# A four-layer graph network on one core: the same operations in new orders on all engines, with new PSUM banks

## The reference

```python
x = _layernorm(x + L0(x, nodemask, adj, adj, W_qkv, W_out, b_out))   # attention
x = _layernorm(x + L1(x, adj, W1, b1, gamma, beta, W2, b2))          # hypergraph convolution, twice
x = _layernorm(x + L2(x, adj, Wv, bv, aw, ab, Wk, bk))               # gated transition, applied K-1 times
x = _layernorm(x + L3(x, adj, W))                                    # mean over neighbours, then a linear map

# L0, 8 heads of 64
attn = softmax(where(m2, q @ k.T * scale, -big)) * 0.33
attn = attn + 0.33 * where(m2, adj, 0) + 0.33 * exp(-where(m2, adj, big))
out  = (attn @ v) @ W_out + b_out
# L1: conv(z, W, b) = Dn * (H @ (Be * (H.T @ (z @ W.T)))) + b, H = (adj != 0)
h = layer_norm(relu(conv(x, W1, b1)), gamma, beta); out = conv(h, W2, b2) + x
# L2
e = leaky_relu(sj + si + ab); T = adj * exp(e) / rowsum
out = relu(x @ Wk[0] + (T @ x) @ Wk[1] + (T @ T @ x) @ Wk[2] + sum(bk))
# L3
out = relu(concat(x, (adj @ x) / deg) @ W.T)
```

## Time and profile before

| | us |
|---|---|
| median of 3 runs | 1377.84 |
| lowest and highest run | 1376.25, 1380.79 |
| profiled execution, device time | 1377.72 |
| its span, first to last instruction | 1375.8 |
| PE busy | 1290.7 (94%) |
| DVE busy | 1075.6 (78%) |
| ACT busy | 956.0 (69%) |
| POOL busy | 550.1 (40%) |

### The profile page before, as it was taken

One profiled execution on the slowest core, in us unless ns is written; L12 is line 12 of the kernel. 1 busy time (PEld: TensorE's weight loads), 2 busy tenths in 40 slices (PEclk: granted clock), 3 DMA queues, 4 the chain that ended last, 5 costly groups with the idle time before them and its releaser, 6 DMA issues.

```text
span 1375.8 us, 32640 instructions
## 1 busy us (share of the span) xinstructions
PE 1290.7 (94%) x9577; PEld 1111.6 (81%) x9577; DVE 1075.6 (78%) x3291; ACT 956.0 (69%) x2806; POOL 550.1 (40%) x1221
## 2 busy tenths in 40 slices
PE   4799999999999999999999999999999999999985
PEld 3678888888888888888888888888888888888863
DVE  2568878888887887887888878888888778888873
ACT  3467767777777777777777777677777777777753
POOL 3034434344443444443334444344444434444432
PEclk8899999999999999999999999999999999999997
DMA  6000000000000000000000010000001000000000
GB/s 192 11 16 25 24 16 16 23 17 24 24 15 24 16 21 19 24 24 15 24 16 16 24 24 20 19 16 23 17 24 24 15 24 16 19 21 24 16 8 8
DMA packets 44292, 32.51 MB, mean 24 GB/s; under 512 B 8176, under 2 KB 43120, under 8 KB 44272
## 3 DMA queue, kind: packets, MB, share of 16 engines
q1 hardware_dynamic: 42688, 31.47, 8.1%
q0 software_dynamic: 176, 0.52, 0.2%
q10 hardware_dynamic: 1408, 0.27, 0.1%
HBM read 23.87 MB, written 8.39 MB: 23 GB/s over the span
## 4 chain that ended last, share of the span: by engine, by line
PE 29%; POOL 22%; issue 19%; DVE 16%; ACT 9%; POOLq 1%; ACTq 1%; DVEq 0%; DMA 0%; SPq 0%
POOL rs L1520 9%; PE PS L400 4%; PE PS L522 4%; PE PS L401 4%; PE PS L404 4%; POOL rs L1526 3%; POOL rs L1516 3%; DVE ysb L1287 3%; PE PS L532 3%; POOL ys L1533 3%; ACT qk L817 2%; DVE ysb L1279 2%; DVE st L1291 2%; DVE ys L1169 2%; POOL gate L1541 2%
## 5 line engine op out<-in xcount | busy, mean ns | idle before, releaser
L1520 POOL TENSOR_TENSOR rs<-rs,mhalf 128x1 f32<-128x1 f32 x320 | 180.0, 562 | 25.4
L834 ACT ACTIVATE prob<-PS,neg_max 128x128 f32<-128x128 f32 x512 | 179.5, 413 | 1.8 <-DVE neg_max L1145 1.8
L1158 DVE SCALAR_TENSOR_TENSOR prob<-prob,rl,gate 128x128 f32<-128x128 f32 x512 | 160.1, 372 | 0.2
L852 ACT ACTIVATE x<-ysb,rs 128x256 f32<-128x256 f32 x128 | 78.3, 612 | 104.3 <-POOL rs L1526 104.3
L478 PE MATMUL PS<-xT_hi,wqk_hi 128*128 128x256 f32 x512 | 139.5, 294 | 9.0 <-DVE wk_lo L1071 4.8
L1574 POOL TENSOR_TENSOR z<-z,bk_bc 128x256 f32<-128x256 f32 x64 | 48.1, 751 | 236.7 <-ACT z L902 236.7
L479 PE MATMUL PS<-xT_hi,wqk_lo 128*128 128x256 f32 x512 | 136.4, 287 | 0.0
L834 ACT ACTIVATION_READ_ACCUMULATOR prob<-PS,neg_max 128x1 f32 x512 | 129.8, 253 | 0.0
L1516 POOL TENSOR_TENSOR rs<-mv,eps_c 128x1 f32<-128x1 f32 x256 | 54.2, 212 | 186.3 <-DVE mv L1081 186.3
L1192 DVE SCALAR_TENSOR_TENSOR hid<-PS,Dn,b_bc 128x512 f32<-128x512 f32 x64 | 48.1, 751 | 82.8 <-PE PS L404 82.8
L478 PEld LDWEIGHTS PS<-xT_hi,wqk_hi 128*128 128x128 f32 x512 | 99.9, 195 | 11.3 <-issue 5.0
(11 more groups left out here) (213 smaller groups left out, 4280.8 us busy)
## 6 DMA issues: line engine op xcount, KB each, us to landing
xin<-in_x_dram SPq DMA_DIRECT2D x32, 256.0 KB, 2.8
out_dram<-xout SPq DMA_DIRECT2D x32, 256.0 KB, 2.2
adj_in<-in_adj_dram SPq DMA_DIRECT2D x32, 128.0 KB, 2.1
wrow<-in_adj_dram SPq DMA_DIRECT2D x32, 128.0 KB, 4.6
wqkv_raw<-in_L_gnn_W_qkv_dram SPq DMA_DIRECT2D x1, 1536.0 KB, 7.7
w_raw<-in_L_gnn_W_dram SPq DMA_DIRECT2D x3, 512.0 KB, 11.9
mask_bc<-in_nodemask_dram SPq DMA_DIRECT2D x32, 32.0 KB, 2.9
wk_raw<-in_L_gnn_Wk_dram SPq DMA_DIRECT2D x3, 256.0 KB, 8.7
```

What stands on the lines that cost most here:

```text
L834: last = act.activation(prob[:, t, h, :], PS[:, bank, k * P:(k + 1) * P], ACT.Exp, bias=neg_max[:, t, h:h + 1], accum_out=row_sum[:, t, h: ...
L852: act.activation(dst, src, ACT.Identity, scale=rs[:, n, g, 1:2], bias=rs[:, n, g, 0:1]).then_inc(done, 1)
L1158: last = dve.scalar_tensor_tensor(prob[:, t, h, :], prob[:, t, h, :], rl[:, t, h:h + 1], gate[:, t], ALU.mult, ALU.add)
L1520: return pool.tensor_tensor(rs[:, n, g, 1:2], rs[:, n, g, 0:1], mhalf[:], ALU.pow)
```

## The change

All 23 settings of PSUM banks are new. The order of items changes in group on PE, ACT, DVE and POOL; SP's is as it was. No item is added or dropped, and no item's own code changes. Waits of the form after(...) are dropped where they were for the old banks and others are put in for the new ones. The diff, cut to its core:

```diff
-        bank_adjT = 7
-        bank_xT0 = 7
-        bank_qk = (0, 3, 1, 7)
-        bank_v = (3, 0)
-        bank_S = (1, 5)
+        bank_adjT = 4
+        bank_xT0 = 1
+        bank_qk = (3, 0, 0, 2)
+        bank_v = (4, 5)
+        bank_S = (6, 2)
...
-        bank_h = (6, 4)
-        bank_hT = (0, 4)
-        bank_y1 = (4, 0)
+        bank_h = (2, 5)
+        bank_hT = (1, 1)
+        bank_y1 = (0, 6)
...
 # PE
                 if B:
-                    after(pe, dve_o3, 2, s - 2, 2)
                     h_(j, 0)
-                if F:
+                    h_(j, 1)
+                if F:
+                    after(pe, dve_hb, 2, s - 1, 1)
                     qk_(i, 3)
                 if B:
-                    h_(j, 1)
-                if F:
-                    after(pe, act_qk, 4, s, 3)
+                    hT_(j, 0)
+                if F:
                     S_(i, 0)
-                if B:
-                    hT_(j, 0)
-                if F:
                     S_(i, 1)
                 if B:
+                    after(pe, dve_hT, 2, s - 1, 1)
                     hT_(j, 1)
                     hw_(j, 0)
                     hw_(j, 1)
                     y1_(j, 0)
+                    after(pe, act_exp, 4, s, 2)
                     y1_(j, 1)
-                if F:
-                    v_(i, 0)
-                    after(pe, dve_y1, 2, s - 1, 2)
-                    v_(i, 1)
                 if L:
                     xT0_(n)
+                if F:
+                    v_(i, 0)
+                    v_(i, 1)
                 if B:
                     xT2_(j)
...
                 if F:
                     PV_(i, 0)
                 if B:
+                    after(pe, act_E, 4, s - 1, 4)
                     T1_(j, 0)
+                if F:
+                    after(pe, dve_xT0, 1, s + 1, 1)
+                    PT_(i, 1)
+                if B:
+                    T1_(j, 1)
                 if L:
-                    after(pe, act_E, 4, s - 1, 4)
-                    after(pe, act_v, 2, s, 2)
                     qk_(n, 0)
                 if B:
-                    T1_(j, 1)
-                if F:
-                    PT_(i, 1)
-                if B:
-                    after(pe, act_qk, 4, s + 1, 1)
                     T2_(j, 0)
+                if F:
+                    PV_(i, 1)
+                if B:
+                    T2_(j, 1)
                 if L:
                     qk_(n, 1)
-                if B:
-                    T2_(j, 1)
-                if F:
-                    after(pe, dve_o2, 2, s - 1, 1)
-                    PV_(i, 1)
+                if F:
+                    after(pe, dve_OT, 2, s, 1)
                     W_(i, 0)
...
 # DVE, after the first hb_
                     hb_(0)
-                    hb_(1)
                     bnh_(0)
                     mvh_(0)
+                    hb_(1)
+                    hT_(0)
+                    degb0_()
+                    bnh_(1)
                 if F:
                     max_(0)
...
 # POOL
                 if B:
                     resid_(0)
                     resid_(1)
+                    rsh_(0)
+                    aT_()
+                if F:
+                    fresid_()
+                if B:
+                    rsh_(1)
                 if F:
                     gate_()
-                if B:
-                    rsh_(0)
-                    rsh_(1)
-                    aT_()
-                if F:
-                    fresid_()
```

More of the change, by code:

```diff
@@ L684, in group @@
                 if F:
-                    after(pe, act_exp, 4, s, 2)
+                    after(pe, act_exp, 4, s, 4)
                     PT_(i, 0)
@@ L938, in group @@
                 if B:
-                    relu_(j, 0)
-                    aT_(j)
+                    hT_(j, 0)
                 if F:
@@ L973, in group @@
                 if B:
-                    al_(j, 1)
+                    Z01_(j, 1)
                     Y_(j, 0)
-                if L:
-                    qk_(n, 0)
-                if B:
-                    Y_(j, 1)
                 if F:
@@ L982, in group @@
                 if B:
-                    x3_(j, 0)
+                    Y_(j, 1)
+                if L:
+                    qk_(n, 0)
                 if F:
                     OT_(i, 1)
+                    carry(i)
+                if B:
+                    x3_(j, 0)
                 if L:
@@ L1348, in group @@
                 if B:
-                    hT_(0)
-                    bnh_(1)
                     mvh_(1)
                     hT_(1)
+                    degb_()
                     hw_(0)
@@ L1376, in group @@
                 if F:
-                    Dsum_(0)
+                    norm_(1, 0)
                 if B:
                     Z_(0)
-                if L:
-                    front(n)[1]()
                 if F:
+                    rl_(1, 1)
                     norm_(1, 1)
@@ L1385, in group @@
                     gmax_(0)
+                    al_(0)
                     Z_(1)
[L1387 removed]
+                if L:
+                    after(dve, pe_v, 2, s, 2)
+                    front(n)[1]()
+                if B:
+                    all_(0)
                     z2_(0)
[L1389 to L1390 removed]
                     gmax_(1)
                     al_(1)
+                    z2_(1)
                     den_(0)
                     rden_(0)
+                    all_(1)
                     Y_(0)
[L1396 removed]
+                    den_(1)
+                    rden_(1)
+                    Y_(1)
+                    Yl_()
                 if F:
@@ L1441, in group @@
                     y3_(0)
-                    o3_(1)
-                    bn3_(0)
-                    mv3_(0)
-                    y3_(1)
                 if F:
@@ L1448, in group @@
                 if B:
+                    bn3_(0)
+                    o3_(1)
+                    mv3_(0)
+                    y3_(1)
                     bn3_(1)
```

109 lines of the change are left out of this document (49 added, 60 removed).

## The result

The changed kernel takes 1362.93 us (median of 4 runs, 1359.42 to 1364.37), the kernel before 1379.05 us beside it (4 runs, 1376.25 to 1380.79): a ratio of 0.9881 with a 95% interval of 0.9855 to 0.9908. A second measurement gave 0.9889 (0.9868 to 0.9910). So it is 16 us faster where 9 were forecast; 1363 lies in the range of 1350 to 1391. The profiled execution took 1362.91 with a span of 1361.1; that of before had 1375.8, so 14.7 us are to be found.

What follows compares the result with a forecast made beforehand. It took a latency cycle through all engines, meeting an almost full PE, as the bound. The last gain to bind, 0.28 us a pass over 31 passes, made 8.7 us: 1377.8 - 8.7 = 1369, range 1350 to 1391.

Steps and rivals of the forecast that it cites:

- Step 1: End of the pass on DVE: bn3_(0) ahead of o3_(1) brings mv3_(0) about 0.3 us earlier, out_(j, 1) near 3.2.
- Step 7: Middle and end of the pass: new waits end 0.1 to 0.5 us before PE comes; T3_, ax_ keep their distance.
- Steps 2 and 3: Heads of ACT and PE: relu_(j, 0) directly behind mask_, hT_(j, 0) before S_; hT_(j, 1) at 8.97, gain 0.34 us.
- Step 4: y1_(j, 1) on PE at 13.27 against 13.49, gain 0.22 us; the new act_exp wait hidden.
- Step 5: x load: fresid_ ends at 10.6, load lands near 13.65, PE there at 13.62; just in time, no reserve.
- Its rival: Slower by the x load: fresid_ ending after about 11.1 makes passes longer, 1390 us; chance 0.20.
- Step 6: xT2_ and Z_: x2_(j, 1) at 17.2 against 17.48, Z_ at 18.98 against 19.26; gain 0.28 us a pass.
- The sum: Step 6's gain of 0.28 us a pass over 31 passes, 8.7 us in all, giving 1369 us.
- left at nothing: Set-up and last, half-empty group: costs of 0.9 and gains of 0.3 us, together under 1 us, counted as zero.
- norm_ over POOL's z: DVE's norm_ ends before POOL's addition, which falls on gmax_ and al_; al_(0) perhaps 0.4 us late, sum unchanged.

Runs made afterwards that it cites:

- b_tail_new: The kernel before with only DVE's end-of-pass order changed (bn3_(0) ahead of o3_(1), Dn_ ahead of both): 1367.24 us, ratio 0.9920 to before.
- a_tail_old: The changed kernel with DVE's end-of-pass order put back to the old one: 1372.97 us, ratio 0.9961 to before.
- a_y1bank: The changed kernel with other banks for y1_(j, 1), xT0_ and the first graph's Z01, so y1_(j, 1) need not wait for exp_(i, 0): 1360.22 us, ratio 0.9869 to before.
- a_pool_old: The changed kernel with POOL's old order, fresid_ behind the gates: 1451.03 us, ratio 1.0519 to before.
- best2: The changed kernel with DVE-order and bank edits in first and last pass, and xT0_ behind both v_ on PE: 1358.36 us, ratio 0.9866 to before.

## Why the prediction was right in direction and small in size

- **Step 1** had the mechanism and half the size. It said 0.3 us for mv3_(0) from DVE's order; that part alone gave 0.36 and 0.39 us a pass. The rest of the change, which b_tail_new and a_tail_old separate from it, brought mv3_(0) forward by another 0.22. What the forecast left out is on PE: adjT_ behind T3_(j, 1), which the rows give the same 0.22. Step 7, "T3_ and ax_ keep their distance to the end", is where it failed: ax_ does (0.81 us before the new pass), T3_(j, 1) does not.
- **Steps 2 and 3** held. relu_(j, 0) directly behind mask_, hT_(j, 0) at t = 5.70 without a wait, then S_, then hT_(j, 1); each 0.22 to 0.37 early, which is step 1's 0.28 and, from S_(i, 1) on, the 0.1 by which S_(i, 0) is shorter than the 1.22 taken (682.40 to 683.52). The short wait for relu_ that was expected ahead of hT_(j, 0) is not there. The cover over the new wait on dve_hT held in the full passes; in the last one, without it, PE waits 1.84 us for hT_(j, 1).
- **Step 4** failed in its detail (the wait on act_exp is 0.40 us and visible), with no effect on the sum (a_y1bank).
- **Step 5** held within 0.12 us, xT0_ at 13.50 for 13.62. Its rival's mechanism is real (a_pool_old), and its price lacked the clock.
- **Step 6** gave 0.28 where 0.65 was measured. It was taken as the smallest of several gains. As all the items hang on the same mv3_(0), it is the shift of that one item, and this was mis-sized: 0.3 for the 0.58 that mv3_(0) moved.
- **The sum.** 31 x 0.28 = 8.7 should have been 31 x 0.66 = 20.4 for the full passes, and the half-empty ones, "left at nothing", cost 3.5 or a little more (the first) and 2.4 (the last). The two errors have opposite signs, so the total is nearer to the forecast than its terms are, which is luck.
- **norm_ over POOL's z.** The four operations of the earlier trace rows are gone as an outlier: a norm_ operation takes 346 ns in the mean, 372 before (DVE is busy with the 512 of them for 142.7 us against 160.1), and y2_, which stood over POOL work too, 425 instead of 598. The Trainium skill (SBUF — State Buffer, § "SBUF: two separate sides") had this as whole instructions excluding each other; the trace agrees in direction, and no run here isolates its part of the 0.658. The delay that the forecast derived from it for al_(0) did not come: al_'s two operations start at 698.05 and 698.37 and take 0.28 and 0.29 us, mostly ahead of the POOL addition at 698.52.

## What to carry to other kernels

When a loop is a latency cycle through all engines, find the item that every later item hangs on, and add up all that stood ahead of it, on the engine itself and on the engine it waits for; here a statistic on VectorE gave 0.36 us and, as the rows have it, two transposes on TensorE 0.22, and the pass followed their sum nearly one for one. A visible wait is no price until something moves it: one of 0.40 us a pass was worth nothing, while a load with no reserve was free when released at 10.5 and cost 2.96 us a pass at 13.0, nearly a third of it through the clock, which fell at about every second of its waits. Orders and banks tuned for the full pass should be read again for the first and the last one, where the cover of other work is gone.

## What the runs showed of the hardware

- The granted clock of TensorE fell in a pause of 2.6 to 4.3 us in one piece, or just behind it, in the first pass of eleven traces, and in the other three did not after pauses of 1.1 and 1.3, or 1.4, 0.4 and 1.5 us. Behind pauses of 2.1 to 2.4 us in a_pool_old it fell about every second time. Sixteen matmuls took 1.98 us at the lower level and 1.09 at the higher, and a pass of a_pool_old 43.5 us with such a fall and 41.9 without. How long it stays down varies: in the changed kernel the windows 58:62 and 62:66 show 0.59 and 0.56, in best2, with a pause of 2.73 us, 0.82 and 0.76. Why stays open.
- The same last pass took 39.25 and 41.45 us in two kernels, with a mean granted clock of 0.83 and 0.79 as the visible difference. Differences of 1 to 3 us between kernels of equal pass length are of this kind or from the set-up, and no verdict here rests on them.
- Four VectorE operations with two SBUF inputs took 1.62 us over a GpSimd addition and 1.11 us elsewhere; one of 128x256 took 598 ns in the mean where some lay over GpSimd work and 425 where none did (y2_).
